# Three graph convolutions: the gathered rows in a ring of 14 slots instead of 7

## The chip, the cores and the metric

One core of a Trainium2 chip runs the whole program. The metric is the device time of one execution in microseconds (us); the time of a kernel is the median of its runs. The profile is one further execution, recorded instruction by instruction.

The engines are TensorE (PE, with its weight loads as PEld), VectorE (DVE), ScalarE (ACT), GpSimd (POOL) and SyncE (SP). Here POOL issues the indirect DMAs that gather rows by index, and SP keeps the bookkeeping of the ring.

## What is computed

A graph with 6250 nodes of 128 features and 100000 edges, the edges sorted by destination, goes through four residual blocks. The reference, cut down:

```python
x = x + attention(relu(layernorm(x)), src, dst, ...)          # 8 heads
x = x + gine(relu(layernorm(x)), src, dst, edge_attr_16, ...) # 4 layers
# two GCN convolutions, then one linear convolution:
norm = dinv[row] * dinv[col]
h   = relu(segment_sum((h   @ W1)[row] * norm[:, None], col) + b1)
out = relu(segment_sum((h   @ W2)[row] * norm[:, None], col) + b2)
x = x + out
x = x + segment_sum(h[src] @ W, dst) + h @ W_self
```

The change is in the last three sums, the convolutions: each gathers, for every edge, the 128 features of its source node and adds them up per destination node.

## The kernel before

The 100000 edges are padded to 196 chunks of 512 (four columns of 128). The nodes are 49 windows of 128, in 7 groups of 7. As the edges are sorted by destination, a chunk belongs to one window or to a few neighbouring ones. The work of a pass is a list of 245 steps (0 to 244): each step is one pair of chunk and window, and the next step moves on to the next window or to the next chunk. Tables made at the start tell for each step its slot in the ring, how many chunks it needs, its window and whether a group ends there. All engines walk this list four steps to a loop turn (UNROLL, 61 turns).

A convolution pass (k = 6, 7, 8) runs as follows.

POOL (`gather_pass`, lines 850 to 883) issues for each chunk four indirect DMAs, one for each column of 128 edges; each brings 128 rows of 512 bytes from the node table in HBM into the chunk's slot. Before the first of them it waits until `slot_free` tells that the slot may be written. After the third gather of a chunk it waits for the landing of the chunk before and then raises `rows_ready` for that one (`tell_rows`, line 862).

TensorE (`conv_steps`, `sum_rows`, lines 1191 to 1218) waits for `rows_ready` of the step's chunk and for `onehot_ready`, the mark of the step. It then adds up the chunk's rows per node of the window with four fp32 matmuls (eight instructions in the trace) into one of four PSUM banks. The last matmul raises `segsum_ready`.

VectorE (`sum_pass`, lines 1720 to 1757) waits for `segsum_ready` of the step, adds the bank to the window's sum (line 1746) and makes the mark of the step four ahead (`mark_step`, line 1715). So TensorE can be at most four steps ahead of VectorE. At the end of a group VectorE, TensorE and ScalarE also do the dense part for its seven windows.

SP (`chunk_pass`, kind "rows") hands out the ring. At the start of a pass it waits until the last pass is stored and raises `slot_free` seven times (line 694). After that it reads from the table `free_at` the step after which each chunk is no longer needed, waits for `segsum_ready` to reach it, and raises `slot_free` (line 713). So POOL is at most seven chunks ahead of what TensorE has signalled.

The three passes run one after the other, since each gathers what the last one stored. The layers before them (k = 2 to 5, line 1119 and 1126) use the same ring `rows`, and a second one, `gates`, which lies in `q_res`, the place of the attention's queries. The convolutions don't use `q_res`.

## Time and profile before

| | us |
|---|---|
| median of 3 runs | 10520.3 |
| the runs | 10517.32 to 10532.23 |
| the profiled execution | 10607.1 |
| its span | 10605.0 |
| first convolution, first gather to last | 7111 to 8245 |
| second convolution | 8271 to 9407 |
| third convolution | 9438 to 10576 |

| engine | busy us | share of the span |
|---|---|---|
| POOL | 6216.3 | 59% |
| PE | 5675.4 | 54% |
| DVE | 3028.2 | 29% |
| ACT | 949.0 | 9% |

The profiled execution is 0.8% longer than the median of the others. In a timeline row the first two numbers are the start and the duration in us, "x8" is a count of instructions, and the brackets say how long the engine was idle before and what ended that ("remote" where no instruction of the trace could be found at that moment, "issue" where the engine waited for nothing that the profile shows). In a row of a group, "mean ns" is the duration of one instruction, and after the second bar stands the idle time of the engine just before them, with its releasers. The times of starts are recorded; the ends of matmuls are modelled.

### The profile page before, as it was taken

What the parts mean: (1) busy time and instruction counts of PE and PEld (TensorE: products, weight loads), DVE (VectorE), ACT (ScalarE), POOL (GpSimd) and SP (SyncE); (2) the same over time, 40 slices, a digit from 0 to 9 for tenths busy, and PEclk for the clock granted to TensorE, in tenths of its full rate; (3) what the DMA queues carried; (4) which work ended last, traced back from release to release, by engine and by line L of the source; (5) the groups of instructions that cost most, each with busy time, mean ns of one, the idle gap of its engine ahead of it and who ended that gap; (6) DMA issues with size and microseconds to landing.
All of it is one profiled execution on the core that took longest, in us unless ns stands there. A gap on an engine that the chain in (4) does not pass through costs nothing.

```text
span 10605.0 us, 107124 instructions
## 1 busy us (share of the span) xinstructions
PE 5675.4 (54%) x23750; PEld 3922.0 (37%) x23751; DVE 3028.2 (29%) x7366; ACT 949.0 (9%) x1767; POOL 6216.3 (59%) x6738
## 2 busy tenths in 40 slices
PE   3566637566775667656675666653334333333334
PEld 2333437333443334433343333333333333333234
DVE  3444577212221122312222122331122112231222
ACT  1111100111111111101111111110000000000000
POOL 3655536565555655466554655546666666656665
PEclk7566659777887788878788778875566556665666
DMA  5777755332323323233332323221111111111111
GB/s 167 218 219 218 203 139 155 90 88 82 85 75 86 87 82 85 79 85 87 83 83 75 88 81 81 77 59 45 47 49 48 46 46 49 48 46 46 47 49 47
DMA packets 796948, 945.08 MB, mean 89 GB/s; under 512 B 269045, under 2 KB 530448, under 8 KB 796302
## 3 DMA queue, kind: packets, MB, share of 16 engines
q0 software_dynamic: 213408, 463.35, 16.4%
q1 hardware_dynamic: 474970, 390.60, 13.2%
q10 hardware_dynamic: 108436, 89.99, 2.6%
q14 instruction: 128, 1.05, 0.0%
q8 instruction: 6, 0.10, 0.0%
HBM read 797.55 MB, written 152.25 MB: 90 GB/s over the span
## 4 chain that ended last, share of the span: by engine, by line
another core or an unknown queue 44%; PE 18%; issue 13%; DVE 9%; DVEq 3%; POOL 0%; SPq 0%; ACT 0%; DMA 0%; ACTq 0%; POOLq 0%
PE ps_big L1119 8%; PE ps_seg L1126 5%; DVE onehots L1715 2%; DVE sums L1746 2%; DVEq L453 1%; PE ps_seg L1197 1%; PE ps_big L1197 1%; PE ps_big L1063 1%; PE ps_t L1038 1%; DVE gate L1894 1%; DVE h_res L1898 0%; DVE group_stats L1783 0%; PE ps_seg L1063 0%; PE ps_big L987 0%
## 5 line engine op out<-in xcount | busy, mean ns | idle before, releaser
L871 POOL DMA_INDIRECT rows<-node_rows,idx_all x5488 | 5209.8, 949 | 3470.5 <-SPq L713 1590.0
L1119 PE MATMUL ps_big<-rows,ident 128*128 (+1 forms) x1960 | 1221.8, 709 | 1386.0 <-DVE onehots L1715 1249.5
L1746 DVE TENSOR_TENSOR sums<-sums,ps_seg 128x128 f32 x1342 | 385.5, 287 | 5141.3 <-remote 3368.8
L1126 PEld LDWEIGHTS ps_seg<-onehots 128*128 128x128 f32 x7840 | 1206.0, 223 | 899.0 <-issue 735.5
L1126 PE MATMUL ps_seg<-onehots 128*128 128x128 f32 x7840 | 1236.4, 309 | 260.6 <-issue 168.0
L1715 DVE SCALAR_TENSOR_TENSOR onehots<-ps_mm,away 128x512 f32<-128x512 f32 x1975 | 1349.3, 684 | 21.4 <-issue 13.8
L1197 PE MATMUL ps_seg<-rows,onehots 128*128 (+1 forms) x2952 | 613.8, 372 | 1235.4 <-DVE onehots L1715 595.8
L1119 PE MATMUL ps_big<-q_res,ident 128*128 (+1 forms) x1960 | 1153.9, 674 | 150.9 <-issue 123.0
L1119 PEld LDWEIGHTS ps_big<-rows,ident 128*128 128x128 f32 x1960 | 412.0, 224 | 2036.2 <-DVE onehots L1715 1461.7
L871 POOL DMA_INDIRECT sums<-kv_rows,idx_all x784 | 743.4, 948 | 548.2 <-SPq L711 281.2
L1197 PEld LDWEIGHTS ps_seg<-rows,onehots 128*128 128x128 f32 x2952 | 536.7, 272 | 1301.7 <-DVE onehots L1715 619.0
L1197 PE MATMUL ps_big<-rows,onehots 128*128 x2928 | 585.4, 371 | 723.5 <-issue 410.1
L1399 ACT ACTIVATE onehots<-ps_big 128x512 f32<-128x512 f32 x980 | 582.7, 597 | 4301.1 <-remote 2008.5
L1197 PEld LDWEIGHTS ps_big<-rows,onehots 128*128 128x128 f32 x2928 | 538.2, 278 | 763.8 <-issue 465.3
L987 PE MATMUL ps_big<-q_res,onehots 128*128 x1960 | 426.2, 387 | 269.1 <-issue 141.9
L987 PEld LDWEIGHTS ps_big<-q_res,onehots 128*128 128x128 f32 x1960 | 380.1, 289 | 422.2 <-issue 422.2
L998 PE MATMUL ps_mm<-w_edge,attr_t 65*128 65x512 f32 x392 | 327.4, 932 | 295.1 <-ACT attr_t L1288 219.8
L1746 DVE TENSOR_TENSOR sums<-sums,ps_big 128x128 f32 x366 | 103.7, 283 | 1259.2 <-remote 993.0
L1119 PEld LDWEIGHTS ps_big<-q_res,ident 128*128 128x128 f32 x1960 | 347.7, 220 | 177.4 <-issue 171.8
L1341 ACT COPY nodes<-ps_t 128x512 f32<-128x512 f32 x112 | 56.5, 534 | 3525.7 <-remote 1947.9
L1601 DVE SCALAR_TENSOR_TENSOR onehots<-rows,node_id,ps_seg 128x512 f32<-128x512 f32 x246 | 269.8, 1097 | 278.0 <-issue 206.9
L1626 DVE TENSOR_TENSOR onehots<-ps_big,sums 128x512 f32<-128x512 f32 x245 | 167.9, 685 | 418.1 <-remote 299.1
(215 smaller groups left out, 2974.4 us busy)
## 6 DMA issues: line engine op xcount, KB each, us to landing
q_res<-gates_by_edge SPq DMA_DIRECT2D x784, 256.0 KB
rows<-node_rows,idx_all POOLq DMA_INDIRECT x5488
rows<-dst_padded SPq DMA_DIRECT2D x196, 256.0 KB
value_rows_by_edge<-sums SPq DMA_DIRECT2D x196, 256.0 KB
gates_by_edge<-gate ACTq DMA_DIRECT2D x196, 256.0 KB
rows<-value_rows_by_edge SPq DMA_DIRECT2D x196, 256.0 KB, 3.5
node_rows<-h_res ACTq DMA_DIRECT2D x49, 448.0 KB
sums<-kv_rows,idx_all POOLq DMA_INDIRECT x784
```

Source lines behind the costliest of these rows:

```text
L453: eng.load(regs, table[0:1, ds(i, 1), columns].rearrange("a i n -> a (i n)"))
L871: pool.indirect_dma_start(target[:, r, j, :], None, table, bass.IndirectOffsetOnAxis(ap=idx_all[:, c * J + j:c * J + j + 1], axis=0), elem ...
L987: last = nc.tensor.matmul(ps_big[u][:, j * D:j * D + D], onehot_t[:, u, j, :], q_res[:, ds(row.get(WIN_, WINDOWS), 1), :].rearrange("p w d ...
L998: nc.tensor.matmul(ps_mm[1 - u][:, :], attr_t[0:J * ED + 1, 1 - u, :], w_edge[0:J * ED + 1, :, :].rearrange("p j d -> p (j d)"), start=Tru ...
L1119: last = nc.tensor.matmul(ps_big[u][:, :], ident[:, :], chunk_words(source, slot, 0, CHUNK), start=n == 0, stop=n == 1)
L1126: last = nc.tensor.matmul(ps_seg[u][:, 0:D], onehots[:, u, j, :], msg[:, u, j, 0:D], start=j == 0, stop=j == J - 1)
L1197: last = nc.tensor.matmul(seg_four[u][:, 0:D], onehots[:, u, j, :], chunk_words(rows, slot, j * D, D), start=j == 0, stop=j == J - 1)
L1399: nc.scalar.activation(msg[:, u, :, 0:D], ps_big[u][:, :].rearrange("p (j d) -> p j d", d=D), ACT.Relu)\
L1601: V.scalar_tensor_tensor(onehot_t[:, u, :, :].rearrange("p j e -> p e j"), dst_rows[:, ds(slot, 1), :].rearrange("p s (e j) -> p (s e) j", ...
L1626: V.tensor_tensor(prod, ps_big[u][:, :].rearrange("p (j d) -> p j d", d=D), kv_rows[:, ds(slot, 1), :, 0:D].rearrange("p s j d -> p (s j) ...
L1715: V.scalar_tensor_tensor(onehots[:, u, :, :], numbers.rearrange("p (a n) -> p a n", a=1).to_broadcast([P, J, P]), 0.0, away[:, ds(at, J)]. ...
L1746: V.tensor_tensor(mine, mine, seg_four[(n - 1) % depth][:, 0:D], ALU.add).then_inc(agg_added, 1)
```

## The change

The rows of the convolutions go into a ring of 14 slots. Its place is one tile `stock`, which holds the former `q_res` and `rows` side by side: the seven new slots lie in the last seven slots' worth of the queries' place, the seven old ones follow.

What follows from it:

- SP frees 14 slots at the start of a pass and then one for each chunk, in its new function `conv_slots`: a loop of 26 turns of seven chunks that reads seven words of `free_at` each.
- POOL gathers in `gather_wide`, with the same four gathers for a chunk and the same place of `tell_rows`; the slot is c % 14, with one landing semaphore for each of the 14.
- TensorE reads the slot from a second table of turns, `row_turns` with 10 words, in place of `row_words` with 12. SP loads it with four DMAs after the last layer, and TensorE waits for them once (`words_loaded`).
- VectorE computes that table of slots in the set-up (five instructions), and SP stores it.
- `gates_landed` and `values_landed` become one set of semaphores, `slot_loaded`, which makes room for the new ones.
- Each step of TensorE still raises `segsum_ready`, and VectorE still marks four steps ahead.

```diff
     RING = 7
     GROUP = 7
-    assert CHUNKS % RING == 0 and WINDOWS % GROUP == 0
+    WIDE = 2 * RING
+    assert CHUNKS % RING == 0 and CHUNKS % WIDE == 0 and WINDOWS % GROUP == 0
...
-        q_res = sb("q_res", [P, WINDOWS + 1, D])
+        SLOT = J * COLS
+        Q_WORDS = (WINDOWS + 1) * D
+        stock = sb("stock", [P, Q_WORDS + RING * SLOT])
-        rows = sb("rows", [P, RING * J * COLS])
-        SLOT = J * COLS
+        rows = stock[:, Q_WORDS:Q_WORDS + RING * SLOT]
+        wide_rows = stock[:, Q_WORDS - (WIDE - RING) * SLOT:Q_WORDS + RING * SLOT]
+        wide_ring = wide_rows.rearrange("p (s k) -> p s k", s=WIDE)[:, :, 0:CHUNK].rearrange("p s (j d) -> p s j d", j=J)
+        assert (WIDE - RING) * SLOT <= Q_WORDS
         slots_of = lambda flat: flat[:, 0:RING * SLOT].rearrange("p (s k) -> p s k", s=RING)[:, :, 0:CHUNK]\
...
+        ROW_TURN = 10
+        words_at = 2 * GROUP_WORDS
+        row_turns = score_words[0:1, words_at:words_at + TURNS_ * ROW_TURN].bitcast(i32)\
+            .rearrange("a (i n) -> a i n", n=ROW_TURN)
...
-        gates_landed = [sem(f"gates_landed{r}") for r in range(RING)]
-        values_landed = [sem(f"values_landed{r}") for r in range(RING)]
+        wide_landed = [sem(f"wide_landed{r}") for r in range(WIDE - RING)] + rows_landed
+        slot_loaded = [sem(f"slot_loaded{r}") for r in range(RING)]
...
+            sp.wait_ge(table_made, 2)
+            sp.dma_start(wide_d.rearrange("(g p) -> p g", p=P), wide_of[:, :]).then_inc(table_stored, 16)
...
+            sp.wait_ge(table_stored, 32)
+            by_turn = lambda field, first, turns, count: words_d[field:field + 1, first:first + turns * UNROLL]\
+                .rearrange("a (i n) -> a i n", n=UNROLL)[:, :, 0:count]
+            for to, source in (
+                (row_turns[0:1, :, 0:4], wide_d[BEFORE + 1:BEFORE + 1 + LAST].rearrange("(a i n) -> a i n", a=1, n=UNROLL)),
+                (row_turns[0:1, :, 4:8], by_turn(COUNT_, BEFORE + 1, TURNS_, 4)),
+                (row_turns[0:1, :, 8:9], by_turn(ENDS_, 0, TURNS_, 1)),
+                (row_turns[0:1, :, 9:10], by_turn(ENDED_, 0, TURNS_, 1)),
+            ):
+                sp.dma_start(to, source).then_inc(words_loaded, 16)
+            def conv_slots(k):
+                begun = N_STEP * sum_no(k)
+                wait_alone(sp, "sp", group_stored, (k - 1) * (16 * GROUPS))
+                wait_alone(sp, "sp", segsum_ready, begun)
+                for r in range(WIDE):
+                    sp.sem_inc(slot_free, 1)
+                def free_turn(turn):
+                    freed, regs = load_free(turn * RING - WIDE, RING)
+                    for r in range(RING):
+                        sp.wait_ge(segsum_ready, freed[r] + begun).then_inc(slot_free, 1)
+                    for reg in regs:
+                        sp.free_register(reg)
+                with engine_loop(sp, 2, TURNS) as turn:
+                    free_turn(turn)
             for n in range(3):
-                k = CONV_PASS + n
-                chunk_pass(k, "rows", segsum_ready, N_STEP * sum_no(k))
+                conv_slots(CONV_PASS + n)
...
+            def gather_wide(k, table, part_):
+                uses = (k - CONV_PASS) * (CHUNKS // WIDE)
+                landed_before = (0, (LAYERS + 1) * (CHUNKS // RING) * (16 * J))
+                def tell_rows(c):
+                    pool.wait_ge(wide_landed[c % WIDE], landed_before[c % WIDE // RING] + (uses + c // WIDE + 1) * (16 * J)).then_inc(rows_ready, 1)
+                for c in range(CHUNKS):
+                    wait_alone(pool, "pool", slot_free, (k - 1) * CHUNKS + c + 1)
+                    for j in range(J):
+                        pool.indirect_dma_start(
+                            wide_ring[:, c % WIDE, j, :], None, table,
+                            bass.IndirectOffsetOnAxis(ap=idx_all[:, c * J + j:c * J + j + 1], axis=0),
+                            element_offset=part_ * (NP * D)).then_inc(wide_landed[c % WIDE], 16)
+                        if j == J - 2 and c > 0:
+                            tell_rows(c - 1)
+                tell_rows(CHUNKS - 1)
             with pool.Fori(0, LAYERS // 2) as two:
                 for n in range(2):
                     gather_pass(two * 2 + (L1_PASS + n), tables, n, gated=True)
             for n in range(3):
-                gather_pass(CONV_PASS + n, tables, (LAYERS + n) % 2)
+                gather_wide(CONV_PASS + n, tables, (LAYERS + n) % 2)
...
-                        last = nc.tensor.matmul(seg_four[u][:, 0:D], onehots[:, u, j, :], chunk_words(rows, slot, j * D, D),
+                        last = nc.tensor.matmul(seg_four[u][:, 0:D], onehots[:, u, j, :], chunk_words(wide_rows, slot, j * D, D),
...
-                    with clamped(pe, words[5:5 + UNROLL], 1, CHUNKS) as counts:
+                    with clamped(pe, words[4:4 + UNROLL], 1, CHUNKS) as counts:
...
-                        slot = up_to(words[n - 1], (RING - 1) * SLOT)
+                        slot = up_to(words[n - 1], (WIDE - 1) * SLOT)
                         pe.wait_ge(rows_ready, landed[n - 1])
                         for j in range(J):
-                            pe.lower_ap(chunk_words(rows, slot, j * D, D))
+                            pe.lower_ap(chunk_words(wide_rows, slot, j * D, D))
                         sum_rows(slot, n % 4, marked[n - 1])
...
-                each_turn(pe, "pe", row_words, slice(0, 12), conv_steps)
+                if i_conv == 0:
+                    pe.wait_ge(words_loaded, 16 * (WORD_LOADS + TURN_LOADS))
...
+            divide(cf[:, 0, :], WIDE, None, slot_f)
+            V.tensor_scalar(wide_of[:, :], slot_f, float(SLOT), None, ALU.mult).then_inc(table_made, 1)
```

## Rows read from the trace of the kernel before

**Rows 1.** The page: its span, and the group of the table gathers.
```profile
span 10605.0 us, 107124 instructions
...
L871 POOL DMA_INDIRECT rows<-node_rows,idx_all x5488 | 5209.8, 949 | 3470.5 <-SPq L713 1590.0
```

**Rows 2.** Windows, line 871, first and third pass: POOL busy (count), clock, DMA.
```profile
7111.00:8245.00 1134.00, 744.34 (x784) 0.59 0.18 48
...
9438.00:10576.00 1138.00, 742.61 (x784) 0.61 0.18 48
```

**Rows 3.** Waits of POOL, passes 1, 2 (two rows), 3: total us, times, longest.
```profile
POOL rows L871 <- SPq L713: 155.4, 47, 5.6
POOL rows L871 <- SPq L713: 155.9, 50, 5.6
POOL rows L871 <- SPq L694: 26.9, 1, 26.9
POOL rows L871 <- SPq L713: 168.7, 60, 7.3
```

**Rows 4.** Groups by line, the three passes, 7111 to 10576 us.
```profile
L1197 PE MATMUL ps_seg<-rows,onehots 128*128 (+1 forms) x2928 | 610.2, 373 | 1235.4 <-DVE onehots L1715 595.8 <-issue 543.7 <-POOLq L862 94.1
L1197 PE MATMUL ps_big<-rows,onehots 128*128 x2896 | 579.7, 372 | 715.7 <-issue 410.1 <-DVE onehots L1715 272.8 <-POOLq L862 31.9
L1746 DVE TENSOR_TENSOR sums<-sums,ps_seg 128x128 f32 x362 | 103.7, 286 | 1364.4 <-remote 1050.5 <-issue 216.5 <-PE ps_seg L1197 68.3
L1746 DVE TENSOR_TENSOR sums<-sums,ps_big 128x128 f32 x360 | 102.0, 283 | 1250.1 <-remote 984.0 <-issue 137.4 <-PE ps_seg L1197 100.9
```

**Rows 5.** Groups by line in the attention pass, 1547 to 1902 us.
```profile
L1850 DVE TENSOR_TENSOR sums<-sums,ps_seg 128x137 f32 x122 | 35.9, 295 | 63.0 <-PE ps_seg L1063 47.4 <-issue 15.4
L1850 DVE TENSOR_TENSOR sums<-sums,ps_big 128x137 f32 x122 | 35.9, 294 | 12.6 <-PE ps_big L1063 8.7 <-DVE group_stats L1822 1.7
```

**Rows 6.** Timeline of TensorE and VectorE, inside the second pass.
```profile
8811.50 2.07 PE L1197 MATMUL ps_big<-rows,onehots 128*128 x8 [2.87 <-issue]
8819.10 0.29 DVE L1746 TENSOR_TENSOR sums<-sums,ps_seg 128x128 f32 x1 [14.60 <-remote]
8820.05 2.07 PE L1197 MATMUL ps_seg<-rows,onehots 128*128 x8 [6.47 <-issue]
8833.81 0.29 DVE L1746 TENSOR_TENSOR sums<-sums,ps_seg 128x128 f32 x1 [13.82 <-remote]
8836.03 0.29 DVE L1746 TENSOR_TENSOR sums<-sums,ps_big 128x128 f32 x1 [1.33 <-remote]
```

**Rows 7.** Timeline of POOL in the same stretch.
```profile
8828.71 0.95 POOL L871 DMA_INDIRECT rows<-node_rows,idx_all  x1 [0.31 <-issue]
8834.62 0.95 POOL L871 DMA_INDIRECT rows<-node_rows,idx_all  x1 [4.96 <-SPq L713]
```

**Rows 8.** Table of windows of the same stretch, line 1746 alone.
```profile
8794.90:8800.90 6.00, 1.41 (x5) 0.67 0.18 44
8800.90:8829.70 28.80, 0.58 (x2) 0.58 0.20 52
```

**Rows 9.** Waits of POOL in the first 74 us of the second pass.
```profile
POOL rows L871 <- SPq L713: 8.4, 2, 4.6
```

**Rows 10.** Timeline of POOL and VectorE at the end of the second pass.
```profile
9405.38 0.95 POOL L871 DMA_INDIRECT rows<-node_rows,idx_all  x1 [0.30 <-issue]
9409.01 0.29 DVE L1746 TENSOR_TENSOR sums<-sums,ps_big 128x128 f32 x1 [6.93 <-remote]
9417.45 0.28 DVE L1746 TENSOR_TENSOR sums<-sums,ps_big 128x128 f32 x1
```

**Rows 11.** Timeline of VectorE in the set-up.
```profile
64.76 0.17 DVE L1536 TENSOR_SCALAR div_i<-cf 128x2 int32<-128x2 f32 x1
64.96 0.17 DVE L1537 TENSOR_SCALAR div_i<-div_i 128x2 int32<-128x2 int32 x1
```

**Rows 12.** DMA issues, first 300 us: queue, count, size, us to landing.
```profile
step_words_by_field<-word SPq DMA_DIRECT2D x1, 5.0 KB, 12.1
```

More of the change, by code:

```diff
@@ L48, in build_program @@
     ROWS = 2 * UNROLL
-    assert LAST % UNROLL == 0 and GROUP >= UNROLL
+    assert LAST % UNROLL == 0 and GROUP >= UNROLL and LAST // UNROLL % 2 == 1
     assert CHUNKS <= 255 and RING <= 7 and WINDOWS < 63 and WINDOWS // GROUP < 8
@@ L369, in build_program @@
         GROUPS = WINDOWS // GROUP
+        TURN_LOADS = 4
         def wait_alone(eng, name, semaphore, value):
@@ L907, in weigh @@
                     wait_alone(pool, "pool", weights_loaded[half], (pair + 1) * 16)
-                wait_alone(pool, "pool", values_landed[r], (pair * 2 + half + 1) * 16)
+                wait_alone(pool, "pool", slot_loaded[r], (pair * 2 + half + 1) * 16)
                 nc.gpsimd.tensor_copy(vals[:, r, :, D:D + HEADS],
@@ L1217, in conv_steps @@
                         if part is not None:
-                            with pe.If(words[10] != 0), clamped(pe, words[11:12], 0, GROUPS - 1) as group:
+                            with pe.If(words[8] != 0), clamped(pe, words[9:10], 0, GROUPS - 1) as group:
                                 part(group[0])
                 parts = {1: conv_turn, 2: conv_sum} if i_conv < 2 else {1: conv_turn, 2: conv_self, 3: conv_sum}
-                each_turn(pe, "pe", row_words, slice(0, 12), conv_steps)
+                if i_conv == 0:
+                    pe.wait_ge(words_loaded, 16 * (WORD_LOADS + TURN_LOADS))
+                each_turn(pe, "pe", row_turns, slice(0, 10), conv_steps)
                 for n in sorted(parts):
```

12 lines of the change are left out of this document (8 added, 4 removed).

## The prediction

> **What bounds the kernel now.** I read the page first. The line that matters is the gathers of the node table on POOL [rows 1]: 5488 of 949 ns each, with 3470 us of idle time before them, of which 1590 us end when SP frees a slot. The change touches 2352 of these, in the last three passes, so I looked at those passes alone.
>
> Each pass takes 1134 to 1138 us from its first gather to about its last [rows 2]. On the timeline a gather starts every 1.25 us while POOL is not held (0.95 us and 0.30 us between two, the bracket in rows 7), so a chunk costs 4 x 1.25 = 5.0 us and 196 chunks 980 us. What is left, some 155 us in each pass, is POOL's wait for a slot: 155.4, 155.9 and 168.7 us [rows 3]. Together that is 480 us, 4.6% of the kernel. This is the only thing that a longer ring can take away, and on a first look it is just what a longer ring is for.
>
> Then I asked why the seven slots are full. If TensorE were short of rows, the groups of its step would show waits for POOL. They show 94.1 + 31.9 = 126 us for that, and 595.8 + 272.8 = 869 us for VectorE's marks [rows 4]. VectorE in turn is idle for 1364.4 + 1250.1 = 2614 us before 722 of its additions, 3.6 us for each, nearly all put down to "remote" or "issue" [rows 4]. It waits for `segsum_ready`, TensorE's signal. The timeline shows the case: TensorE runs a step at 8811.50 us, done by 8813.6; VectorE's next addition comes at 8819.10 after 14.60 us, the one after that at 8833.81 after 13.82 us [rows 6]. In between TensorE runs one step, at 8820.05, as soon as the mark of the first addition is there. After 8822.1 it runs nothing, so the signal that lets VectorE go at 8833.81 is at least 11.7 us late.
>
> When does it learn? POOL had been issuing since 8794.9 without a stop of any length. It stops at 8829.66 for want of a slot [rows 7]; 4.1 us later the signal is there, VectorE adds, and 0.8 us after that POOL has its slot and goes on. The table of windows of this stretch shows five additions in the first 6 us after POOL's restart and two in the next 28.8 us [rows 8]. And in the attention pass, where POOL issues no gathers and TensorE and VectorE do the same kind of step, VectorE waits 63.0 + 12.6 us for 244 additions, 0.31 us each [rows 5]. I take from this: while POOL issues gathers back to back, TensorE's signals come late, and they come in a bunch once POOL has stood still for about 4 us. What holds them the trace does not tell. The stops of POOL are then not only a cost. They are what moves the other engines.
>
> **The change part by part.** *Seven more slots in the steady state.* One gather stream needs a step every 5.0 x 196 / 245 = 4.0 us to go on for ever. Past its first 6 us it gets one in 28.8 / 2 = 14.4 us [rows 8]. A ring of any size fills up at that ratio: it gains a chunk every 5.0 us and loses one every 18. Once 14 slots are full, POOL stops as before, waits the same 4 to 5 us, gets one slot back, restarts, and has the 6 us in which five or so additions pass. The same number of steps per stop, so the same number of stops. More rows at hand would help only if TensorE lacked rows in these first 6 us; its 126 us of such waits in three passes [rows 4] are the upper bound for that, and I take nothing of it, since what it does after the 6 us is held up again. Cost 0, gain 0.
>
> *The first fill.* In the second pass POOL has two waits in its first 74 us, 8.4 us in all [rows 9]. At 5.0 us a chunk, (74 - 8.4) / 5.0 = 13 chunks are issued in that time, so both come before chunk 14, and a ring of 14 holds up none of these. In three passes: -3 x 8.4 = -25 us. This is the part of the change that I trust.
>
> *The end of a pass.* What POOL gains on TensorE must still be worked off after the last gather. Now the last gather ends at 9406.3; the signals come 2.7 us later, and nine additions run from 9409.01 to 9417.45, so 8.44 / 8 = 1.06 us for a step [rows 10]. With 14 slots up to seven chunks more wait then, 7 x 1.25 = 9 steps, 9 x 1.06 = 9.5 us. Bounds: 0 if the ring is hardly fuller than seven, and 9 x 2.07 = 19 us if TensorE runs each step at the long duration of rows 6 (clock 0.58, rows 8, so mostly 1.2 GHz). I take 5 us, a ring half fuller, three times: +15 us.
>
> *The set-up.* Five small instructions on VectorE, start to start 0.20 us [rows 11]: +1 us, since the weights' copies queue right behind them. SP's store of the slots is one more small scattered DMA; the nearest one takes 12.1 us to land [rows 12], and nothing needs it before the first convolution. It is queued ahead of the stores of keys and values, which wait for TensorE anyway. If that cover were gone it would be under half a microsecond.
>
> *Tables, loops, semaphores.* SP's four loads for the new table are issued after the last layer's sums. POOL's first gather of the second pass waits 26.9 us for SP, since the last pass has to be stored [rows 3]; the first convolution has the same wait, in which four loads of some 12 us lie. If they didn't fit, they would cost at most 12 us once. TensorE loads 10 words a turn for 12, SP seven for eight, POOL issues the same waits and gathers: 0. The merged semaphores change no wait.
>
> **The sum.** Against the profiled execution: -25 + 15 + 1 = -9 us on 10607.1. That execution is 0.8% above the median, and terms of this size scale with nothing, so I set them against the median: 10520 - 9 = 10511 us. The likeliest case's own range is 10480 to 10540.
>
> **Rivals.** *The ring absorbs the waits.* If the signals are held for a limited time (some 30 us at most) rather than for as long as POOL streams, or if an arriving signal brings all the others with it, then 14 slots, 70 us of gathers, outlast any hold. Then the 480 us [rows 3] go, less 3 x 9.5 us at the ends: 10520 - 480 + 29 = about 10070 us. If half of the stops stay, 10290 us. For it: signals do pass now and then while POOL streams, as at 8819.10 [rows 6], and the stretch of rows 8, 35 us, is as long as seven slots allow without more signals, so what happens at 60 or 70 us isn't shown. Against it: the ratio of 14.4 us to 4.0 us in rows 8. Chance 0.2.
> The Trainium skill, "TensorE: Matmul & The Clock Gate", section "The cost: per-tile semaphore tail", puts an increment on a matmul at some 26 ns. By that rule signals would never be the limit, and the outcome would be that of this rival; the 13.82 us of rows 6 speak against it. The skill's "Perfetto Trace Analysis", section "Tensor Engine Instruction (MATMUL, LD_WEIGHTS)", says that the end of a matmul is an estimate, so the lateness might lie in the matmul and not in its signal. That would not change the sum.
>
> *Longer streams hold the signals longer.* A stop is now also a service to TensorE, and the wider ring puts it off: at the start of a pass to chunk 14 or later, up to 35 us later than now, with four steps finished and TensorE standing still. The steps pile up, and the pass pays at its end, 19 us at the slow duration, with the stops as many as before since each lets only five or six steps pass. That is 3 x 19 = +57 less what the first fill saves if it saves half, -12: 10565 us. It decides where stops per pass stay at 47 or more. For it: in 28.8 us of streaming only two steps passed [rows 8]. Against it: at the end POOL is out of the way, and steps run at 1.06 us [rows 10]. Chance 0.2.
>
> **How the numbers follow.** Likeliest case 0.55, absorbing 0.2, piling up 0.2, anything else 0.05. A measurement of this kernel can tell about 0.2%, 21 us, from no change. The likeliest case lies within that three times in four, else on the fast side; the second is faster; the third is slower in four of five. So faster 0.34, same 0.46, slower 0.20. For 8 in 10 the range takes in the near part of the absorbing case and most of the third: 10330 to 10570 us.
>
> **What will show it.** In the likeliest case POOL's waits on SP's freeing line are 430 to 480 us in three passes, with a first one only after chunk 14; TensorE's waits for POOL's telling line shrink towards nothing; those for VectorE's marks stay near 870 us; POOL's wait between two passes, now 26.9 us [rows 3], grows by 5 to 10 us. If POOL's waits fall under 300 us, the step "a ring of any size fills up" is wrong, and so is my prediction. If VectorE's mean idle time before an addition falls well under 3.6 us, the signals are less late than I think, whatever the time does.

## The result and the profile after

The changed kernel takes 10577.2 us in the median of five runs (10569.6 to 10600.4), the kernel before, timed beside it, 10517.3 us (10499.1 to 10532.2). The ratio is 1.0066 with a 95% interval of 1.0051 to 1.0081: 0.66% slower. I had forecast 10511 us, no change. The range ended at 10570 us, 7 us short of the result.

The page's span and the waits of POOL in the three convolution passes, one query for each pass (total us, times, longest us), of the changed kernel:

```profile
span 10575.3 us, 107141 instructions
...
POOL stock L980 <- SPq L841: 154.7, 50, 9.8
POOL stock L980 <- SPq L836: 55.0, 1, 55.0
...
POOL stock L980 <- SPq L841: 156.4, 40, 9.8
POOL stock L980 <- SPq L836: 39.6, 1, 39.6
...
POOL stock L980 <- SPq L841: 153.8, 42, 9.7
POOL stock L980 <- SPq L836: 54.1, 1, 54.1
```

L841 is SP's freeing of a slot in mid-pass, L836 its first grant at the start of a pass. The waits in mid-pass are nearly what they were: 154 to 156 us in each pass, where [rows 3] has 155.4, 155.9 and 168.7 us. The wait at the start of the second pass, which holds the end of the first, was 26.9 us [rows 3] and is 39.6 us. The groups by line over the three passes (7055 to 10530 us) say the same of the other engines:

```profile
L1262 PE MATMUL ps_seg<-stock,onehots 128*128 (+1 forms) x2880 | 566.6, 358 | 1096.0 <-issue 579.3 <-DVE onehots L1784 442.2 <-POOLq L975 71.6
L1262 PE MATMUL ps_big<-stock,onehots 128*128 x2856 | 553.1, 363 | 967.9 <-issue 492.9 <-DVE onehots L1784 474.6
...
L1815 DVE TENSOR_TENSOR sums<-sums,ps_seg 128x128 f32 x356 | 101.8, 286 | 1173.4 <-remote 822.3 <-issue 220.1 <-PE ps_seg L1262 90.6
L1815 DVE TENSOR_TENSOR sums<-sums,ps_big 128x128 f32 x356 | 100.8, 283 | 1472.0 <-remote 1197.7 <-issue 159.9 <-PE ps_seg L1262 61.1
```

TensorE's waits for rows shrank from 94.1 + 31.9 = 126 us [rows 4] to 71.6 us. In either kernel 66 to 67 us of that are the waits of the three passes' first steps, which come before the depth of a ring plays a part. What shrank is the waits behind the first steps, from 59 to 5 us. Its waits for marks are 442.2 + 474.6 = 917 us where they were 869, and VectorE is idle for 1173.4 + 1472.0 = 2645 us before 712 additions, 3.7 us for each, where it was 3.6. Mid-pass nothing of size has changed. What has changed is the end. Timeline of POOL, VectorE and TensorE at the end of the second pass:

```profile
9347.62 0.95 POOL L980 DMA_INDIRECT stock<-node_rows,idx_all  x1 [0.30 <-issue]
...
9351.18 0.29 DVE L1815 TENSOR_TENSOR sums<-sums,ps_big 128x128 f32 x1 [2.85 <-remote]
9351.39 0.68 DVE L1784 SCALAR_TENSOR_TENSOR onehots<-ps_mm,away 128x512 f32<-128x512 f32 x1
9351.99 1.15 DVE L2008 TENSOR_TENSOR h_res<-ps_t,dinv 128x512 f32 x2
...
9360.77 1.88 DVE L1863 TENSOR_SCALAR gate<-x_res,group_mv,group_root 128x128 f32 x7
...
9364.42 0.29 DVE L1815 TENSOR_TENSOR sums<-sums,ps_seg 128x128 f32 x1 [1.10 <-issue]
...
9365.36 2.08 PE L1262 MATMUL ps_seg<-stock,onehots 128*128 x8 [10.29 <-DVE onehots L1784]
```

The last gather ends at 9348.6, and 17 additions are still to come where there were nine [rows 10]; the last runs at 9381.8. In between stands the work of a whole group of nodes on VectorE, 9352.0 to 9364.4, for which TensorE waits 10.29 us. In the kernel before, this group's work lay beside gathers, some 33 us ahead of the end of the last one at 9406.3:

```profile
9373.71 1.15 DVE L1939 TENSOR_TENSOR h_res<-ps_t,dinv 128x512 f32 x2
```

To compare kernels I use three sums over the three convolution passes, all from the timelines' start times. **Off the gathers**: the time from a pass's first gather to its last, less 783 x 1.25 us, the pace of [rows 7]; it holds all of POOL's standing still inside a pass (it is less than the waits for slots, each of which takes the place of a usual gap of 0.30 us). **Ends**: from the end of the last gather to the last addition. **Length**: from the first gather of the first convolution to the end of the kernel. The profiled execution of [rows 1] was an unusually long one, so both kernels were profiled once more, on one chip.

| kernel | off the gathers | ends | length |
|---|---|---|---|
| before, first profile | 466 | 12.0 + 11.1 + 12.2 = 35 | 3494 |
| after, first profile | 441 | 25.0 + 33.2 + 31.3 = 90 | 3520 |
| before, second profile | 447 | 10.5 + 7.4 + 10.8 = 29 | 3465 |
| after, second profile | 437 | 25.1 + 32.8 + 31.6 = 90 | 3517 |

By the second profiles 10 us are gained inside the passes, 61 us are lost at their ends, and 8 us in the set-up (the first gather of the kernel starts at 150.8 us, it was 143.1; between the first profiles it is 6 us, 150.8 and 144.7). -10 + 61 + 8 = 59 us; the two executions lie 59.9 us apart.

### The profile page after: what moved, and what is told of

It reads as the page before. It is cut to its first block, busy times and chain, and to the rows that moved or that the text cites. A ratio compares the mean times of both kernels' runs of the same rounds, so it can differ in the third digit from the quotient of the medians.

```text
span 10575.3 us, 107141 instructions
## 1 busy us (share of the span) xinstructions
PE 5596.3 (53%) x23750; PEld 3872.7 (37%) x23751; DVE 3033.2 (29%) x7371; ACT 947.0 (9%) x1767; POOL 6195.5 (59%) x6738
## 3 DMA queue, kind: packets, MB, share of 16 engines
q14 instruction: 126, 1.03, 0.0%
## 4 chain that ended last, share of the span: by engine, by line
another core or an unknown queue 44%; PE 22%; issue 18%; DVE 10%; DVEq 4%; DMA 1%; ACTq 1%; ACT 1%; POOL 0%; SPq 0%; POOLq 0%
PE ps_big L1184 9%; PE ps_seg L1191 5%; DVE onehots L1784 2%; DVE sums L1815 2%; PE ps_seg L1262 2%; PE ps_big L1262 2%; DVEq L467 1%; PE ps_mm L1063 1%; PE ps_t L1103 1%; PE ps_big L1052 1%; PE ps_big L1128 1%; PE ps_seg L1128 1%; DVEq L1670 0%; DVE gate L1963 0%
## 5 line engine op out<-in xcount | busy, mean ns | idle before, releaser
L917 POOL DMA_INDIRECT stock<-node_rows,idx_all x3136 | 2967.1, 946 | 2143.2 <-SPq L729 1061.9
L1184 PE MATMUL ps_big<-stock,ident 128*128 (+1 forms) x3920 | 2250.5, 692 | 1504.4 <-DVE onehots L1784 1162.5
L980 POOL DMA_INDIRECT stock<-node_rows,idx_all x2352 | 2224.3, 946 | 1304.2 <-issue 654.1
L1184 PEld LDWEIGHTS ps_big<-stock,ident 128*128 128x128 f32 x3920 | 761.3, 222 | 2172.4 <-DVE onehots L1784 1354.7
L1262 PE MATMUL ps_seg<-stock,onehots 128*128 (+1 forms) x2952 | 576.5, 357 | 1099.5 <-issue 582.7
L1262 PE MATMUL ps_big<-stock,onehots 128*128 x2928 | 562.9, 361 | 967.9 <-issue 492.9
L1262 PEld LDWEIGHTS ps_seg<-stock,onehots 128*128 128x128 f32 x2952 | 505.4, 258 | 1159.7 <-issue 623.6
L1262 PEld LDWEIGHTS ps_big<-stock,onehots 128*128 128x128 f32 x2928 | 517.4, 269 | 1002.1 <-issue 509.5
L1052 PE MATMUL ps_big<-stock,onehots 128*128 x1960 | 420.8, 384 | 273.5 <-issue 144.8
L1052 PEld LDWEIGHTS ps_big<-stock,onehots 128*128 128x128 f32 x1960 | 377.1, 286 | 423.6 <-issue 423.5
L1670 DVE SCALAR_TENSOR_TENSOR onehots<-stock,node_id,ps_seg 128x512 f32<-128x512 f32 x246 | 270.0, 1098 | 228.6 <-issue 168.4
L957 POOL TENSOR_TENSOR stock<-stock,score 128x512 f32<-128x512 f32 x196 | 206.7, 1055 | 0.0
```

The lines of the kernel that those rows point to most:

```text
L917: pool.indirect_dma_start(target[:, r, j, :], None, table, bass.IndirectOffsetOnAxis(ap=idx_all[:, c * J + j:c * J + j + 1], axis=0), elem ...
L980: pool.indirect_dma_start(wide_ring[:, c % WIDE, j, :], None, table, bass.IndirectOffsetOnAxis(ap=idx_all[:, c * J + j:c * J + j + 1], axi ...
L1052: last = nc.tensor.matmul(ps_big[u][:, j * D:j * D + D], onehot_t[:, u, j, :], q_res[:, ds(row.get(WIN_, WINDOWS), 1), :].rearrange("p w d ...
L1184: last = nc.tensor.matmul(ps_big[u][:, :], ident[:, :], chunk_words(source, slot, 0, CHUNK), start=n == 0, stop=n == 1)
L1262: last = nc.tensor.matmul(seg_four[u][:, 0:D], onehots[:, u, j, :], chunk_words(wide_rows, slot, j * D, D), start=j == 0, stop=j == J - 1)
L1670: V.scalar_tensor_tensor(onehot_t[:, u, :, :].rearrange("p j e -> p e j"), dst_rows[:, ds(slot, 1), :].rearrange("p s (e j) -> p (s e) j", ...
```

## Experiments

Theory T: the time is lost at the ends of the convolution passes, by the ring's depth. Rival S: in the set-up or the layers. Theory H: POOL's back-to-back gathers hold TensorE's signals. Rival L: the steps themselves are late. Other theories are named in the expectations. First the two kernels again.

> The kernel before, once more, for a second set of lengths by pass. Theory T (the loss lies in the three convolutions, at the end of each pass, where a fuller ring is worked off): the four layers and all before them take what they take in the changed kernel, the three convolutions some 25 to 55 us less (from the first gather of the first to the end about 3460 to 3495 us, against 3520 us), and 9 or 10 additions follow each pass's last gather. Rival S (set-up and layers cost more in the changed kernel): the convolutions take the same 3520 us within 15 us, and the part before them is 40 us shorter than 7055 us.

> The changed kernel once more. Theory T: the convolutions take 3505 to 3530 us again, POOL's waits for slots 430 to 460 us, 16 to 20 additions after each last gather, the last of them 25 to 33 us behind it. Rival S: the convolutions vary by more than the 26 us between the two first profiles, so that these said nothing.

10521.9 and 10581.8 us. Their sums are in the table above.

**Is it the depth?** The changed kernel, SP hands out seven of its 14 slots:

```diff
-                for r in range(WIDE):
+                for r in range(RING):
-                    freed, regs = load_free(turn * RING - WIDE, RING)
+                    freed, regs = load_free(turn * RING - RING, RING)
-                with engine_loop(sp, 2, TURNS) as turn:
+                with engine_loop(sp, 1, TURNS) as turn:
```

> The changed kernel with one thing undone: SP hands out only seven of the 14 slots, so POOL is again at most seven chunks ahead; memory layout, tables, loads, semaphores and set-up stay as changed. Theory T: as fast as the kernel before within 0.15% (10505 to 10535 us), 9 or 10 additions after each last gather, the first wait of POOL at chunk 10. Rival S: the loss stays, 10560 to 10590 us, with the same tail of nine additions.

Ratio to before 1.001 [1.0001, 1.002]: some 0.56 of the 0.66% are the depth. Off the gathers 445, ends 9.5 + 4.7 + 11.3 = 25, length 3459 us, all nearly as before. What is left fits the set-up, where the first gather is again at 150.8 us.

**Four and ten slots**, with the same edit (the first grants and the offset 4 or 10, and one short load for the slots between):

> The changed kernel, but SP hands out only four of its 14 slots. Theory T (the number of stops' steps does not depend on the ring, and the lead of POOL is paid back at the end of each pass): the end of a pass shrinks from the 8 to 9 us at seven slots to about 5 us, the stops stay at 145 to 155 us a pass or grow by 5 us since the first one comes 15 us earlier; time 10500 to 10530 us. Rival R (a short ring leaves TensorE without rows after each restart): stops over 170 us a pass, time above 10570 us, and TensorE's waits for POOL well above the 70 us they have with 14 slots.

> The changed kernel, but SP hands out only ten of its 14 slots. Theory T: between the two measured rings, drains of 15 to 18 us where seven slots have 8 and 14 have 30, so 10535 to 10560 us. Rival P (the loss is a step that comes only with all 14, such as the group's work on VectorE that falls behind the last gather): 10515 to 10530 us, and drains of 12 us at most.

Ratios 1.0012 [1.0001, 1.0023] and 1.0032 [1.0018, 1.0045]; ends 14 and 41 us, off the gathers 485 and 467 us. From here to pause_wide, before itself took 10594 to 10639 us where it was timed beside these kernels, so their times stand against that, and their sums against each other's only roughly. The ends go with the slots, 14, 25, 41, 90 us for 4, 7, 10, 14. The short ring pays 18 us more inside the passes than ten slots do. The steep rise at 14 has a reason of its own: of the four, only 14 slots have it that a group's work lies behind a pass's last gather, and in all three passes. With ten slots 9, 14 and 14 additions follow it and none waits over 2.0 us for the next, with 14 slots (second profile) single intervals are 5.0, 13.2 and 7.6 us. So rival P was right on that part of the price, and wrong that ten slots cost nothing.

**Are the steps slow in themselves?** The changed kernel with gathers for the first 14 chunks of each convolution alone; the other chunks' rows are left out, all steps stay:

```diff
-                    for j in range(J):
+                    for j in range(J if c < WIDE else 0):
...
+                    if c >= WIDE:
+                        tell_rows(c - 1)
```

> The changed kernel, where the three convolutions gather only the first 14 chunks; the other 182 chunks' steps add up the rows that lie in the slots (this part of the computation is left out, everything else of a step is there). It measures TensorE's and VectorE's steps without gathers beside them. Theory H (POOL's back-to-back gathers hold TensorE's signals): after the first 70 us of a pass, VectorE's mean idle time before an addition falls from 3.6 us to under 0.6 us, a step takes 1.0 to 1.5 us, a pass 350 to 480 us instead of 1165 us. Rival L (the lateness is in TensorE's steps themselves, or in the loops of the engines): the idle time stays above 2 us and a pass takes over 700 us.

8343.5 us. Windows of the additions alone, the 14 chunks' gathers and then the rest of the first and of the third pass (VectorE busy, count, clock, DMA):

```profile
7062.10:7131.80 69.70, 1.44 (x5) 0.50 0.20 52
7131.80:7453.40 321.60, 67.92 (x239) 0.95 0.03 9
7932.40:8002.10 69.70, 1.44 (x5) 0.50 0.20 52
8002.10:8325.80 323.70, 67.77 (x239) 0.98 0.03 9
```

Five additions in 69.7 us of gathers, 239 in the 321.6 us behind them, 1.35 us for each. (The second pass takes 375.5 us for its 239. There the work of each of six groups takes 13.2 us from one addition to the next, in the first pass 5.0 us and in the third 6.4 us.) The steps are not slow in themselves; they wait while POOL issues. The granted clock of TensorE is 0.50, its lower level, in the first stretch and 0.95 in the second.

This run doesn't tell whether the matmuls themselves are held up beside gathers or only their signals. The trace of the kernel before does, in the second pass:

```profile
8779.77 4.17 PE L1197 MATMUL ps_seg<-rows,onehots 128*128 x16 [10.58 <-DVE onehots L1715]
8782.89 0.29 DVE L1746 TENSOR_TENSOR sums<-sums,ps_seg 128x128 f32 x1 [0.78 <-issue]
8783.73 2.69 PE L1197 MATMUL ps_big<-rows,onehots 128*128 x16
8786.25 1.06 PE L1197 MATMUL ps_seg<-rows,onehots 128*128 x8
8794.14 0.29 DVE L1746 TENSOR_TENSOR sums<-sums,ps_seg 128x128 f32 x1 [10.36 <-remote]
8794.94 0.95 POOL L871 DMA_INDIRECT rows<-node_rows,idx_all  x1 [3.89 <-SPq L713]
```

Here TensorE runs five steps one behind the other, two in the first row, two in the third, one in the fourth. The addition at 8782.89 takes the first step's sum. The second step's is taken at 8794.14, though TensorE began its next steps at 8783.73 and 8786.25. The starts are recorded times, so for some 10 us it is not the matmuls that are late but the signal. It gets through 3.1 us after POOL's last gather before the stop has ended (8791.05).

**Does each signal have to wait, or all together?** TensorE signals every second step of the convolutions, in either kernel:

```diff
-                    last.then_inc(segsum_ready, 1)
+                    if u % 2 == 1:
+                        last.then_inc(segsum_ready, 2)
...
-                        dve.wait_ge(segsum_ready, upto[n])
+                        if depth == 2 or n % 2 == 1:
+                            dve.wait_ge(segsum_ready, upto[n + (depth == 4)])
```

> The changed kernel, but in the convolutions TensorE signals every second step, with an increment of two, and VectorE waits before every second addition. Theory H1 (each signal that gets through during POOL's back-to-back gathers costs its own hold, some 14 us): each signal now brings two steps, so steps pass at up to twice the rate while POOL streams, POOL's stops in the three passes fall from 436 us to 200 us or less, and the time falls from 10580 to 10350 us or below. Theory H2 (signals are held by time, and one that arrives stands for all that were finished): half as many signals, same stops; POOL's stops stay at 400 to 450 us, and the time is 10560 to 10600 us, since a step may have to wait for its pair. Rival L (the lateness lies in the steps, not in their signals): no change in stops, within 0.2% of the changed kernel.

> The same pairing in the kernel before, with its ring of seven. Theory H1: the stops fall as in the ring of 14 but a ring of seven, 35 us of gathers, rides out fewer holds: stops from 446 us to 200 to 300 us, time 10270 to 10380 us. Theory H2: stops unchanged, 10510 to 10540 us. If the ring of 14 is only harmful, this one is the faster of the two pairings by 40 to 60 us; if a longer ring is of use once signals are rarer, it is the slower.

1.0078 [1.0056, 1.01] and 1.0018 [1.0007, 1.0029]. With half as many signals the time off the gathers is 478 and 479 us, not the half or less of it that H1 wanted, so it is not so much for each signal. H1 fell; H2's times are the nearer ones. The ends of pairs_after are 103 us, 13 more than without pairs.

**How many steps does a stop let through?** A stop is here a place where the starts of two gathers are more than 1.8 us apart. Two, five and six marks and sums in flight where there were four, in the kernel before. The core of six, beside loops of three turns each and longer tables:

```diff
+        sum_banks = seg_four + [ps_mm[1]] + [ps_mm[0]]
+        more_onehots = q_res[:, 0:2 * J, :].rearrange("p (u j) n -> p u j n", u=2)
...
-                sum_pass(k, start_conv, finish_conv, 4, 2 if i < 2 else 4)
+                sum_pass(k, start_conv, finish_conv, 6, 2 if i < 2 else 4)
```

> The kernel before (ring of seven), but the convolutions keep two marks and two sums in flight between TensorE and VectorE where they had four. Theory D (a stop of POOL lets through what TensorE has finished and could not report, which the four places for sums limit to four, and one or two steps more: 244 additions by 42 to 46 stops is 5.3 to 5.8 for each): with two places 3.3 or so pass at each stop, so some 75 stops a pass and 250 to 290 us of them where there were 150, as the layers show now, whose depth is two (68 to 76 stops a pass, 289 us); time 300 to 420 us longer, ratio to before 1.028 to 1.04. Rival Q (the rate at which signals get through is set by POOL's stream alone, and the buffers are wide enough): stops at 145 to 175 us a pass, ratio 1.00 to 1.007.

> The kernel before (ring of seven), but the convolutions keep six marks and six sums in flight, the two more sums in the two PSUM banks that the convolutions do not use, the two more marks in the queries' place; the column numbers that VectorE compares with come from SBUF in the convolutions, and the bodies of TensorE's and VectorE's loops are three turns long. Theory D: 7.3 additions for each stop, 34 stops a pass and some 110 us of them where there were 150; the ends of passes 2 to 3 us longer; time 90 to 120 us shorter, ratio 0.989 to 0.991. Rival Q: stops as before, ratio 0.998 to 1.002. Rival M (the marks become slower with their operand in SBUF): the marks' mean duration over the 0.6 us or so that they take now, which eats the gain.

> The kernel before (ring of seven), but five marks and five sums in flight in the convolutions, the fifth sum in the one PSUM bank that nothing uses there; the numbers for the marks stay in PSUM, and the loops' bodies are five turns long. Theory D: 6.3 additions for each stop, 39 stops a pass and 125 to 130 us of them; time 50 to 75 us shorter, ratio 0.993 to 0.995. Rival Q: ratio 0.998 to 1.002. If six gives nothing and this gives its 60 us, it is the marks' operand that took six's gain; if neither does, the theory falls.

1.0052 [1.0037, 1.0067], 0.9973 [0.9962, 0.9984] and 1.0000 [0.9987, 1.0012]. Stops: 156 in the three passes with two, 122 with five, 97 with six (125 in the second profile of before). For six and five these are about the counts of theory D, 102 and 117, for two it is far off its 225. The time did not follow the counts: off the gathers 511, 462 and 461 us. Rival Q, by which POOL's stream alone sets the rate and the buffers are wide enough, has the ratios of two and five right (1.00 to 1.007, 0.998 to 1.002) and misses that of six narrowly. Fewer stops are longer stops. Over all stops of the second profile of before, and beyond the usual gap of 0.30 us, a stop that follows 3 to 6 us of gathers takes 2.3 us, one that follows 28 to 36 us takes 4.2 us, one after 36 to 50 us 5.3 us. In six some gathers also became slower. POOL's gathers in the convolutions, five and then six:

```profile
L891 POOL DMA_INDIRECT rows<-node_rows,idx_all x2368 | 2238.8, 945 | 1321.2 <-issue 675.9 <-SPq L733 497.4 <-SPq L714 116.2
...
L891 POOL DMA_INDIRECT rows<-node_rows,idx_all x2364 | 2314.7, 979 | 1225.5 <-issue 682.1 <-SPq L733 397.8 <-SPq L714 103.8
```

The waits for slots fell by 100 us, the gathers grew by 34 ns each, 2352 x 0.034 = 80 us. The marks, whose operand came from SBUF in six, did not: 686 against 684 ns. It is the gathers beside a mark that are slow: in six the 619 of them that overlap one take 1073 ns in the mean, the 1720 that touch none 946 ns; in five it is 945 ns for both kinds. So theory D was right on the number of steps in a stop for five and six, wrong for two and wrong on what a stop costs, and rival M named the operand but the wrong engine. Six is the one version that is clearly faster than the kernel before: 10582.8 us beside 10609.8 for before.

**Is it the place of the backlog?** The changed kernel, but for its last 14 chunks POOL may be only five ahead:

```diff
-                with engine_loop(sp, 2, TURNS) as turn:
+                with engine_loop(sp, 2, TURNS - 2) as turn:
                     free_turn(turn)
+                for turn in (TURNS - 2, TURNS - 1):
+                    freed, regs = load_free(turn * RING - 5, RING)
```

> The changed kernel with its ring of 14, but for the last 14 of the 196 chunks SP lets POOL be only five chunks ahead. Theory T with a price by place (an addition that passes at a stop in mid-stream costs POOL 150 / 244 = 0.6 us, most of them being covered by the gathers, and one behind the last gather 1.3 to 1.7 us, all of it uncovered): the ends of passes shrink from 30 to about 5 us, 12 or 13 additions move to stops at 0.6 to 0.8 us each; the three passes gain 45 to 50 us of the 52 they lost, ratio to before 1.001 to 1.002. Rival U (the backlog has to be worked off with POOL standing still wherever it is done): one long stop of 10 to 20 us ahead of the last 14 chunks takes most of the gain, ratio 1.004 to 1.006.

1.0057 [1.0042, 1.0072]. The ends shrink to 8.8 + 9.4 + 4.7 = 23 us, the time off the gathers grows to 524 us, and nothing is gained that the times can tell. POOL at the boundary, in the second pass:

```profile
9369.79 0.94 POOL L986 DMA_INDIRECT stock<-node_rows,idx_all  x1 [22.32 <-SPq L849]
9393.47 0.94 POOL L986 DMA_INDIRECT stock<-node_rows,idx_all  x1 [3.97 <-SPq L849]
```

One stop of 22.3 us (18.5 and 18.8 in the others), against some 4 for the next. Theory T's "price by place" fell; rival U's long stop is there, and its ratio of 1.004 to 1.006 too. The lead is a loan: it is paid back in one piece, at the end or ahead of it.

**Can the standing still be given in small pieces?** A MEMSET of unused memory on POOL behind each gather (1 or 128 columns) or each chunk (784 columns) of the kernel before, and behind each chunk of the changed one:

```diff
+                    pool.wait_ge(paused, next(pause_no))
+                    nc.gpsimd.memset(q_flat[:, 0:pause], 0.0).then_inc(paused, 1)
```

> The kernel before, with one more instruction on POOL behind each gather of the convolutions: a MEMSET of one column (88 ns in the set-up) of unused memory. Theory B (each gather leaves a little of something unserved that goes ahead of TensorE's signals, some 150 / 784 = 0.19 us each, and any time in which POOL issues no gather works it off): the pause takes the place of as much waiting at stops; 784 x 0.09 = 70 us of pauses, or nothing if they fit into the 0.30 us between two gathers, and the stops fall by as much; total within 0.3% of before. Theory H (signals get through only once POOL has stood still for some microseconds): stops as before, 150 us a pass, and the pauses on top: up to 3 x 70 = 210 us more, ratio up to 1.02.

> As the one before, but the MEMSET has 128 columns (194 ns) and a wait for the one before it, so that each gather starts 0.2 to 0.25 us later. Theory B: stops vanish almost wholly, fewer than 10 a pass, a pass takes 784 x 1.47 = 1150 us, TensorE's signals arrive within 1 or 2 us, the ends of passes take under 6 us; ratio 0.998 to 1.004. Theory H: stops of 130 to 150 us a pass stay, 3 x 160 = 480 us on top, ratio 1.03 to 1.045.

> The same pause in one piece, 0.75 us behind each chunk of four gathers. Theory B: as with the small pauses, ratio 0.998 to 1.004 and few stops. Theory H: a pause of 0.75 us is too short to let anything through, so ratio 1.03 to 1.045. If this one helps and the one behind each gather does not, it takes a pause of some length; then the length lies between 0.2 and 0.75 us.

> The pause of 0.75 us behind each chunk in the changed kernel with its ring of 14. Theory B: TensorE keeps up, POOL's lead does not grow, so the ring of 14 is hardly used and the ends of passes take 5 to 10 us where they took 30: ratio to before 0.998 to 1.004 and within 0.2% of the same pause with a ring of seven. Theory H: ratio 1.035 to 1.05, and ends of 25 to 33 us as without pauses.

1.0002 [0.9988, 1.0016], 1.0003 [0.9993, 1.0012], 0.9990 [0.9981, 1.0000] and 1.0054 [1.0036, 1.0071]. POOL's groups in the convolutions, pause_gather and then pause_chunk:

```profile
L874 POOL DMA_INDIRECT rows<-node_rows,idx_all x2383 | 2277.6, 956 | 790.0 <-issue 434.4 <-SPq L714 247.4 <-SPq L695 107.5
L880 POOL MEMSET q_res<- 128x128 f32 x2352 | 520.5, 221 | 34.9 <-remote 31.2 <-issue 1.5
...
L874 POOL DMA_INDIRECT rows<-node_rows,idx_all x2368 | 2244.1, 948 | 876.9 <-issue 628.4 <-SPq L714 142.7 <-SPq L695 105.9
L885 POOL MEMSET q_res<- 128x784 f32 x588 | 452.5, 770 | 0.2
```

Half a millisecond of added instructions costs no time that the runs can tell: the waits for slots, 469 us in the second profile of before, fall to 247 and to 143 us. But not all of it is added standing still, since POOL has a gap of 0.30 us between two gathers anyway. In pause_gather the gathers start 1.335 us apart (the median) instead of 1.25 us, so a MEMSET of 0.22 us holds them up by 0.085 us, 200 us in all. In pause_tiny they still start 1.25 us apart, so its MEMSETs cost nothing because they fit into the gap, and this kernel tests neither theory. Behind a chunk the 0.77 us of pause_chunk hold POOL up by 0.63 us (1.875 us between two starts).

Off the gathers the four have 485, 505, 480 and 473 us, whatever the pieces. That is against the bare theory H, by which stops of some microseconds are needed, and its ratios of 1.03 and more. It fits B's fixed sum, but B wanted fewer than ten stops a pass and ends under 6 us in pause_gather, where 22 to 26 waits a pass are still over 1.8 us and the ends take 8 to 10 us. Nor do pauses alone make the signals prompt: in pause_chunk VectorE still waits 962.8 + 814.6 us on "remote" before its additions. The pauses in the ring of 14 don't spare it its ends, 24.2 + 36.7 + 25.9 = 87 us: POOL still gets its full lead. B's forecast for that one was wrong.

**Both, and half of the gathers.** The pause behind each chunk together with six marks and sums (six_pause); and the kernel before with two of four gathers left out for each chunk of the convolutions, all steps kept:

> The two edits that gave something together, in the kernel before with its ring of seven: six marks and six sums in flight, and a MEMSET of 0.77 us on POOL behind each chunk of a convolution. Theory B (POOL's time without gathers in a pass is a fixed sum, only its pieces can be chosen): 0.996 to 0.999 of before, no more than the two gave alone, 0.9973 and 0.999, and POOL's time off the gathers again 150 to 160 us a pass. Theory H (signals are held while POOL streams; pauses let them through and the deeper buffers let more through with each): the two add up or more, 0.990 to 0.995.

> The kernel before with half of the gathers left out in the convolutions: two of four for each chunk, all steps of TensorE and VectorE as before. Theory B1 (each gather leaves 0.19 us of something that only a pause works off): 392 gathers, 490 us, and 392 x 0.19 = 75 us of stops, a pass of some 585 us, time about 8810 us. Theory B2 (two rates: a step takes 1.36 us while POOL issues nothing, as measured where the gathers were left out, and some 7.7 us, 980 / (236 - 148 / 1.36), while it issues): 490 / 7.7 = 64 steps beside the gathers, 181 x 1.36 = 246 us of stops, a pass of some 750 us, time about 9310 us. Rival H (signals pass only at stops, some five for each stop of 3.4 us, and few while POOL streams): 46 stops of 3.4 us are still needed, a pass of 650 to 670 us, time 9050 us.

six_pause: 0.9993 [0.9983, 1.0003], off the gathers 457, ends 14 us; H's 0.990 to 0.995 fell, B's 0.996 to 0.999 holds within the interval. half: 9099 us, its passes 684, 689 and 682 us. Additions and matmuls of six_pause in the convolutions, then the additions and the gathers of half:

```profile
L1773 DVE TENSOR_TENSOR sums<-sums,ps_seg 128x128 f32 x247 | 71.3, 289 | 860.8 <-PE ps_seg L1223 768.8 <-issue 52.8 <-remote 31.9
...
L1223 PE MATMUL ps_seg<-rows,onehots 128*128 (+1 forms) x1968 | 470.1, 417 | 719.7 <-POOLq L885 620.0 <-issue 70.5 <-DVE onehots L1742 16.5
```

```profile
L1748 DVE TENSOR_TENSOR sums<-sums,ps_seg 128x128 f32 x366 | 105.4, 288 | 613.8 <-PE ps_seg L1199 569.9 <-issue 39.6 <-PE ps_big L1199 3.9
...
L873 POOL DMA_INDIRECT rows<-node_rows,idx_all x1176 | 1120.4, 953 | 970.1 <-DMA rows<-node_rows,idx_all 395.0 <-issue 384.6 <-SPq L694 99.0
```

In six_pause the signals are prompt: VectorE's additions follow TensorE's matmuls ("remote" is 31.9 us where five had 751.1 on the same group), and TensorE waits for rows. POOL itself is the bound there, with its pauses of 0.7 us a chunk and its gathers of 983 ns. So the equal sums off the gathers are not shown to be a law: in six_pause I set the sum by the length of the pause, and may have set it too high. A shorter pause wasn't tried. In half my edit moved the wait for a chunk's landing from behind the third gather of the next chunk to behind its first, which gave POOL 395 us of waits that I hadn't meant. The 173 to 176 us off the gathers in each pass are mostly these, so half doesn't measure the price of a gather, and that H's 9050 us came nearest to its time says little. It does refute B2: with 490 us of gathers it wanted 246 us more, and 176 were enough. B1 against H stays open, and with it what holds the signals.

## Why the prediction was wrong

**What bounds the kernel.** Right: POOL streams, TensorE's signals come late; once shows most plainly that the steps are quick without gathers, and the rows at 8779.77 that it is the signal. Where I wrote that they come "once POOL has stood still for about 4 us", 0.63 us behind each chunk took the place of most stops.

**Seven more slots in steady state, 0.** Right. The waits are 154 to 156 us a pass, and there are 125 stops in the second profile of before, 127 in that of after. The forecast band of 430 to 480 us for the waits was met at 465. The waits for marks were to stay near 870 us and are 917, an addition's mean idle time went from 3.6 to 3.7 us. "The ring absorbs the waits" fell, and so did the outcome that goes with the 26 ns for an increment in the Trainium skill ("TensorE: Matmul & The Clock Gate", section "The cost: per-tile semaphore tail"). As the Trainium skill ("Perfetto Trace Analysis", section "Tensor Engine Instruction (MATMUL, LD_WEIGHTS)") calls the end of a matmul an estimate, I had left open that the matmul rather than its signal is late. The rows at 8779.77, which need only recorded starts, speak against that.

**The first fill, -25.** Between the first profiles it looks exact, 466 to 441, but that is luck: between the second ones it is -10. The first stop comes at chunk 20 and no longer at 10 or 11, as forecast. That the early stops had let steps through, for which later ones must make up, is my reading of it and not shown.

**The end of a pass, +15.** This is the step that failed. It measured +61 (+54 between the first profiles). I took half a ring and 5 us. But the ring was full: by the second profiles 17 + 18 + 20 = 55 additions were left where there had been 8 + 7 + 8 = 23. They run at 1.11 us (the last 16 of each pass, 50.0 us for 45 intervals), near my 1.06, so the 32 more are 36 us, somewhat over the three times 9.5 us that I had set aside as too many. The other part I had not seen at all: the working of a group moved out from beside the gathers, 12.4 us in the second pass (above), and intervals of 5.0 and 7.6 us in the first and the third, 4.2 and 6.8 us beyond an addition's 0.8: together 23 us. 36 + 23 = 59 of the 61 us. I had priced additions only, though the group's work stands in the same loop.

**The set-up, +1.** It measured +8 with the ring of 14 and with seven granted (+6 between the first profiles). The scattered store of the slots' table took 18.5 us to land, where the other one had taken 12.1 [rows 12], and it stands in the queue ahead of the stores of keys and values. VectorE's one wait for these, of before and of after:

```profile
DVE q_res L1588 <- DMA kv_rows<-gate: 16.8, 1, 16.8
...
DVE stock L1657 <- DMA kv_rows<-gate: 21.8, 1, 21.8
```

5.0 us more (14.7 to 20.9 in the second profiles). I had named this place in the queue and called it covered, because the stores wait for TensorE anyway; for this wait the cover was not there. That the new store causes it is read from the traces; no run has it elsewhere.

**The sum.** -9 forecast; -10 + 61 + 8 = +59 measured. I had given 0.20 to a slower kernel. The rival "Longer streams hold the signals longer" had the price, 3 x 19 less 12, and came within 12 us of the result, in part by luck: it priced 19 us an end by slow steps, and what came were more steps at the quick pace and a group's work. Its sign, 47 waits a pass or more, is met only in part: counted as in [rows 3] they are 50, 40 and 42. Its chance of 0.2 was too low, since a ring that fills up at any size must be full at the end of a pass too, and that followed from my own first step.

## What to carry to other kernels

A deeper ring ahead of a consumer that is slower than its producer fills up, and what it holds at the end of each pass is worked off alone (ends of 14, 25, 41 and 90 us here for 4, 7, 10 and 14 slots): price it as a full ring, with all that stands in the consumer's loop, not as its mean step. Before a ring is deepened, find out what lets the consumer go on; if it goes on when the producer stands still, as here, the ring buys nothing. Before a small scattered store is put ahead of others in a queue, look for an engine that waits for one of those: here such a wait grew by 5 to 6 us.

## What was unexpected of the hardware

TensorE's signals pass at 5 in 69.7 us beside POOL's gathers, and its steps take 1.35 us without. The gathers themselves are not late: their packets end 2.2 us after the gather's start in the second profile of before, after 3 us of streaming as after 40. MEMSETs of 0.22 us on POOL behind each gather, 520 us in all, cost no time clear of noise (1.0003 [0.9993, 1.0012]). And gathers took 979 and 983 ns with VectorE's broadcast operand in SBUF, 945 to 956 ns in the kernels that had it in PSUM; in six only those beside a mark were slow, 1073 ns. The runs don't show what is shared in either case.
